# Attention block of a fused LayerNorm + attention + MoE kernel: half of the exponentials go through a fp16 copy on VectorE, and the projections get two PSUM slots each in place of four shared ones

## The chip, the cores and the metric

The kernel runs on all 8 NeuronCores of one Trainium2 chip. Each core takes two of the 16 sequences (4096 tokens) and works alone; no data goes between cores. The metric is the device time in microseconds of the slowest core. Engines are called by the names of the profile: PE (TensorE, matmul), PEld (its weight loads), DVE (VectorE), ACT (ScalarE), POOL (GpSimd) and SP (SyncE); the last two only issue DMAs here.

## The reference

```python
b, s, d_in = x.shape                    # 16, 2048, 1024; 16 heads of 64
q = (x @ Wq.T) ...; k = (x @ Wk.T) ...; vv = (x @ Wv.T) ...
scores = jnp.einsum('bhid,bhjd->bhij', q, k)
scores = scores + jnp.einsum('bhid,ijd->bhij', q, R)          # R: sin/cos of (j - i)
scores = scores + jnp.einsum('hd,bhjd->bhj', u, k)[:, :, None, :]
scores = scores + jnp.einsum('hd,ijd->hij', v, R)[None]
attn = jax.nn.softmax(scores, axis=-1)
ctx = jnp.einsum('bhij,bhjd->bhid', attn, vv)
s = ctx @ Wo.T + bo

gate_logits = xs @ Wg                                          # 8 experts, top 2
h = jax.nn.relu(jnp.einsum('td,edf->etf', xs, W1) + b1)        # d_ff 4096
out_e = jnp.einsum('etf,efd->etd', h, W2) + b2
...
xn = layernorm(x); out = x + attention(xn) * silu(moe(xn))
```

## The kernel before

**Stages.** For each of the two sequences (`b`) the kernel first runs `ln_gate_batch` and then `attention_batch`; after both it runs the MoE (all 8 experts on all tokens, `w1_stage` at L828 and `w2_stage` at L874) and a last stage that joins the two results. Engines follow the program order of their own queue; each wait is a semaphore wait that is written by hand. P, A and V count what PE, ACT and DVE have finished.

**LayerNorm and gate (16 tiles of 128 tokens).** A tile is normalised on DVE, split into a high and a low bf16 part, transposed by PE 128 columns at a time (L307), and brought back to SBUF by ACT (L311, `xnT`) and DVE (L317). 24 small matmuls give the gate logits; a chain of tiny DVE operations and two sigmoids on ACT turn them into the weights `g_wgt` (L374). PE transposes `g_wgt` one tile later, after the next tile's transposes (L327), and ACT copies the result to `wgt_b` (L330).

**Attention, per head pair `hp_i` (8 of them).** (1) K projection: four chunks `ic` of 512 tokens, 8 matmuls each (L465), into `psA_` (ic 0, 1) and `psB_` (ic 2, 3); ACT copies the even head's 64 rows to `Kbuf[0]` (L475), DVE the odd head's to `Kbuf[1]` (L479). (2) `emit_pend`: the previous block's context is normalised (below). (3) DVE prepares `vt` (L485 to L490). (4) Q projection into the same four halves (L505); ACT copies each to one of two buffers `q_sb2` (L517), and DVE makes the rotated query from it, a *rope chain* of ten instructions (L522 to L538) that ends with the last reader of that buffer. (5) On even `hp_i` the V projection of four heads: 16 times 8 matmuls (L560), with ACT copies to `vaug` (L572, L575). Its weights `wvq` come by DMA on the SP queue from `wvbf_hbm`, a bf16 copy of Wv that POOL's first large DMA made in HBM.

**A block.** The four blocks `bi` of a head pair are (head, half of the queries). Each has 16 steps `jt`: scores (two matmuls of 512 columns, L609, into psA for even jt and psB for odd jt), the exponential on ACT over 1024 columns from PSUM (L632), and the context product (two matmuls, L636, into psC or psD in turn). PE's order is scores 0, scores 1, then for each jt: wait for exp(jt), context(jt), scores(jt+2). After step 15 DVE takes the reciprocal of the row sums (L652, one partition by 1024) and ACT copies the context to `ctx_stage` (L657). `emit_pend` broadcasts the reciprocal with two matmuls (L417) and multiplies on DVE (L425); it is called in the next block at jt = 10, or behind the next K projection.

```python
for jt in range(16):
    if jt == 10 and ("pend",) in last:
        emit_pend()
    ...
    p.wait("tensor", A, a_e_l[jt])
    ...
    if jt + 2 < 16:
        pe_s_l[jt + 2] = s_mm(jt + 2)
```

The first block of a head pair waits for rope chains 0 and 1, and for the ACT copy of chunk 3; the second block waits for rope chain 3 (L600 to L603).

## Time and profile before

| what | value |
|---|---|
| time, median of 2 runs | 10926.86 us (10899.97 to 10953.74) |
| profiled execution, its own time | 10124.97 us |
| span of its slowest core (core 2) | 10123.4 us |
| spans of the 8 cores | 10084.0 to 10123.4 us |
| mean granted TensorE clock of the cores | 0.956 to 0.959 |
| PE busy | 8893.5 us (88%) |
| DVE busy | 3470.5 us (34%) |
| ACT busy | 2875.3 us (28%) |

The profiled execution is 802 us (7.3%) below the median of the runs. Every row below comes from the profiled execution, so durations and sums are its own. The span is what lies between the first and the last instruction of the slowest core; it misses 1.6 us of the execution's time. The share of an engine is over the whole span, in which the MoE takes the larger part.

### The profile page before, as it was taken

The page shows a single profiled execution, that of the slowest core. Times are in us where ns is not written, and L with a number is a line of the kernel's source. Part 1 is how long each engine was busy: PE and PEld are TensorE (multiplying, and loading weights), DVE is VectorE, ACT ScalarE, POOL GpSimd, SP SyncE. Part 2 cuts the span into 40 slices and gives each one's busy share as a digit, 9 for nine tenths or more (in the row PEclk, how much of TensorE's full clock was granted, in tenths as well). Part 3 has the DMA queues.
Part 4 walks back from the last instruction along what each step waited for, and adds up shares of the span by engine and source line. Part 5 has one row for each costly group of instructions (what it writes and reads, how often), then busy time and mean ns, then how long its engine had stood idle before and what let it go on. Part 6 is the DMA issues. An engine that isn't in the chain of part 4 may idle for free.

```text
span 10123.4 us, 114688 instructions; the slowest of 8 cores (10084.0 to 10123.4 us)
## 1 busy us (share of the span) xinstructions
PE 8893.5 (88%) x41248; PEld 3938.4 (39%) x41248; DVE 3470.5 (34%) x4945; ACT 2875.3 (28%) x4394; POOL 69.1 (1%) x88
## 2 busy tenths in 40 slices
PE   1577753777789999999999999999999999999995
PEld 1222222222234444444444444444444444444443
DVE  3454444454412222222232222223222322322223
ACT  2466634666421111111112111111211111111111
POOL 0000000000000000000000000000000000000000
PEclk9999976999889999999999999999999999999997
DMA  3000011000032232222223222222322222222215
GB/s 67 30 3 1 1 34 40 3 1 1 24 64 55 59 67 55 55 55 55 56 56 73 55 55 55 55 55 55 67 60 57 57 55 55 55 60 66 55 38 175
DMA packets 381242, 500.10 MB, mean 49 GB/s; under 512 B 10432, under 2 KB 297280, under 8 KB 380632
## 3 DMA queue, kind: packets, MB, share of 16 engines
q1 hardware_dynamic: 308096, 340.04, 10.7%
q0 software_dynamic: 72608, 152.72, 9.7%
q8 instruction: 357, 5.85, 0.2%
q14 instruction: 181, 1.48, 0.0%
HBM read 603.31 MB, written 35.72 MB: 63 GB/s over the span
## 4 chain that ended last, share of the span: by engine, by line
PE 81%; ACT 7%; DVE 6%; issue 3%; DMA 1%; another core or an unknown queue 1%; DVEq 0%; ACTq 0%; SPq 0%; POOLq 0%
PE psH L828 35%; PE psO L874 35%; ACT exp L632 6%; PE psA L609 2%; PE psC L636 2%; PE psD L636 2%; PE psC L560 1%; DMA xo_t<-x 1%; DVE rope L527 1%; PE psB L609 1%; PE psA L465 1%; PE psA L676 1%; PE psB L676 0%; PE psA L307 0%
## 5 line engine op out<-in xcount | busy, mean ns | idle before, releaser
L828 PE MATMUL psH<-xn_tc,W1q 128*128 128x512 bf16 x16384 | 3603.5, 381 | 0.0
L874 PE MATMUL psO<-h_w,W2q 128*128 128x512 bf16 x16384 | 3577.5, 379 | 0.0
L844 ACT ACTIVATE h_sb<-psH,b_c 128x512 bf16<-128x512 f32 x2048 | 1296.7, 684 | 5592.5 <-PE psH L828 5592.5
L828 PEld LDWEIGHTS psH<-xn_tc,W1q 128*128 128x128 bf16 x16384 | 1609.5, 98 | 1958.5 <-issue 60.8
L874 PEld LDWEIGHTS psO<-h_w,W2q 128*128 128x128 bf16 x16384 | 1604.4, 98 | 1936.6 <-issue 15.7
L884 DVE TENSOR_TENSOR acc<-acc,psO 128x1024 bf16<-128x1024 bf16 x1024 | 1250.6, 1221 | 2150.6 <-PE psO L874 2148.0
L848 DVE TENSOR_TENSOR h_w<-h_sb,w_sb 128x512 bf16<-128x512 bf16 x2048 | 870.3, 425 | 2942.4 <-ACT h_sb L844 2939.6
L632 ACT ACTIVATE exp<-psA,cst 128x1024 bf16<-128x1024 f32 x512 | 569.5, 1112 | 157.2 <-PE psA L609 154.9
L632 ACT ACTIVATE exp<-psB,cst 128x1024 bf16<-128x1024 f32 x512 | 567.1, 1108 | 20.3 <-PE psB L609 18.3
L307 PE MATMUL psA<-ident_s,xnhi 128*128 128x128 bf16 x128 | 33.9, 265 | 468.1 <-DVE xnlo L295 374.5
L609 PE MATMUL psA<-Qbuf,Kbuf 128*128 128x512 bf16 x1024 | 311.8, 387 | 141.4 <-ACT q_sb L517 133.0
L636 PE MATMUL psC<-exp,vaug 128*65 128x512 bf16 x1024 | 312.2, 386 | 140.3 <-ACT exp L632 138.5
L636 PE MATMUL psD<-exp,vaug 128*65 128x512 bf16 x1024 | 304.1, 378 | 142.6 <-ACT exp L632 141.4
L652 DVE RECIPROCAL rec_row<-psC 1x1024 bf16<-1x1024 f32 x32 | 209.7, 6552 | 359.0 <-PE psC L636 359.0
L609 PE MATMUL psB<-Qbuf,Kbuf 128*128 128x512 bf16 x1024 | 310.0, 385 | 0.0
L652 DVE RECIPROCAL rec_row<-psD 1x1024 bf16<-1x1024 f32 x32 | 209.7, 6552 | 167.4 <-PE psD L636 167.4
L560 PE MATMUL psC<-wvq,xnT 128*128 128x256 bf16 x1024 | 134.3, 293 | 117.8 <-ACT vaug L572 117.8
L636 PEld LDWEIGHTS psC<-exp,vaug 128*65 128x65 bf16 x1024 | 75.1, 110 | 376.6 <-issue 376.6
L636 PEld LDWEIGHTS psD<-exp,vaug 128*65 128x65 bf16 x1024 | 72.0, 108 | 371.3 <-issue 371.3
L307 PEld LDWEIGHTS psA<-ident_s,xnhi 128*128 128x128 bf16 x128 | 13.3, 104 | 485.3 <-issue 483.9
L609 PEld LDWEIGHTS psA<-Qbuf,Kbuf 128*128 128x128 bf16 x1024 | 97.5, 97 | 263.8 <-issue 164.2
L527 DVE TENSOR_TENSOR rope<-tmpX,psD 32x512 f32<-32x512 bf16 x256 | 175.1, 684 | 27.7 <-DVE rope L527 1.4
(120 smaller groups left out, 2485.4 us busy)
## 6 DMA issues: line engine op xcount, KB each, us to landing
xn_tc<-xnT_scr SPq DMA_DIRECT2D x256, 1024.0 KB, 5.7
W1q<-w POOLq DMA_DIRECT2D x32, 2048.0 KB, 17.9
W2q<-w POOLq DMA_DIRECT2D x32, 2048.0 KB, 34.1
xt<-x SPq DMA_DIRECT2D x32, 512.0 KB, 3.3
xo_t<-x SPq DMA_DIRECT2D x32, 512.0 KB, 12.1
out<-out_t SPq DMA_DIRECT2D x32, 512.0 KB, 11.4
xnT_scr<-xnT POOLq DMA_DIRECT2D x2, 4096.0 KB, 18.3
sT_scr<-Qbuf SPq DMA_DIRECT2D x16, 512.0 KB, 4.0
```

Of the source, the lines that this page charges most:

```text
L465: E.matmul(_ps[:, _o:_o + 512], wkT_b[:, _dt * D + _h * 128:_dt * D + (_h + 1) * 128], xnT[:, _dt * S + _ic * 512: _dt * S + (_ic + 1) * 512],
L527: p.op("vector", lambda E, _ro=r_out, _xs=xs_, _ys=ys_: E.tensor_tensor(rope[_ro:_ro + 32, :], tmpX[_xs:_xs + 32, :], psD_[_ys:_ys + 32, 0 ...
L560: E.matmul(psC_[:, _c:_c + 256], xnT[:, _dt * S + _jt * 128: _dt * S + (_jt + 1) * 128], _w[:, _dt * 256:(_dt + 1) * 256], start=(_dt == 0 ...
L609: E.matmul(_sl[:, _nh * 512:(_nh + 1) * 512], _K[:, _jt * 128:(_jt + 1) * 128], _Q[:, _ig * 1024 + _nh * 512: _ig * 1024 + (_nh + 1) * 512 ...
L632: E.activation(_eb[:], _sl[:], AF.Exp, bias=cst[:, 1:2]))
L636: E.matmul(_pc[0:65, _nh * 512:(_nh + 1) * 512], _va[:, _jt * 65:(_jt + 1) * 65], _eb[:, _nh * 512:(_nh + 1) * 512], start=(_jt == 0), sto ...
L652: E.reciprocal(rec_row[_par][:], _pc[64:65, :]))
L828: E.matmul(_ps[:, _sub * 512:(_sub + 1) * 512], _W[:, _dt * 1024 + _ft * 128:_dt * 1024 + (_ft + 1) * 128], _xb[:, _dt * 512:(_dt + 1) * 512],
L844: E.activation(_hb[:], _ps[:, _sub * 512:(_sub + 1) * 512], AF.Relu, bias=_bb[:, _fq * 8 + _ft:_fq * 8 + _ft + 1]))
L848: E.tensor_tensor(_hw[:, _ft * 512:(_ft + 1) * 512], _hb[:], w_sb[:, _tc * 512:(_tc + 1) * 512], ALU.mult))
L874: E.matmul(_ps[:, _sub * 512:(_sub + 1) * 512], _W[:, _ft * D + _dmt * 128:_ft * D + (_dmt + 1) * 128], _hw[:, _ft * 512:(_ft + 1) * 512], ...
L884: E.tensor_tensor(acc.ap().rearrange("p (dmt t) -> p dmt t", dmt=NDT)[:, _dmg * 2:_dmg * 2 + 2, _tc * 512:(_tc + 1) * 512], acc.ap().rearr ...
```

## The change

The change touches the start, the LayerNorm stage and attention; the MoE and the last stage stay as they are.

- The exponential of odd `jt` is made in two steps: DVE copies the 1024 score columns from PSUM to a fp16 tile `exq` (two of them in turn), and ACT reads that tile. PE still waits for the exponential, as before. Even `jt` is unchanged.
- The K projection uses only the two halves of psA, the Q projection only the two halves of psB. The third and fourth chunk of each wait for the copies of the first and second.
- `q_sb` is one buffer. The copy of the next chunk waits for the whole rope chain of the chunk before.
- The first block of a head pair waits for all four rope chains.
- The HBM copy of Wv is gone. `wvq` is loaded on POOL's queue straight from the f32 input, with the conversion in the DMA.
- The transposition of `g_wgt` and its copy stand at the end of their own tile, not in the next.

```diff
-            p.dma("gpsimd", wvbf_hbm, wvT_d, svb)
...
                     vwg = p.op("vector", lambda E: E.scalar_tensor_tensor(
                         g_wgt[:], g_msk2[:], g_w2[:, 0:1], g_t4[:], ALU.mult, ALU.add), V)
-                    last[("pW",)] = (tt, vwg)
+                    p.wait("tensor", V, vwg)
...
+                    peW = p.op("tensor", lambda E: E.transpose(psW, g_wgt[:], ident[:]), P)
...
             def wv_load(b, qi):
-                p.wait("sync", svb, 16)
                 if ("wvu", qi % 2) in last:
-                    p.wait("sync", P, last[("wvu", qi % 2)])
+                    p.wait("gpsimd", P, last[("wvu", qi % 2)])
                 last[("wvl", qi % 2)] = p.dma(
-                    "sync", wvq[qi % 2].ap().rearrange("p (dt n) -> p dt n", dt=NDT),
-                    wvbf_hbm.rearrange("(dt p) n -> p dt n", p=128)[:, :, qi * 256:(qi + 1) * 256],
+                    "gpsimd", wvq[qi % 2].ap().rearrange("p (dt n) -> p dt n", dt=NDT),
+                    wvT_d.rearrange("(dt p) n -> p dt n", p=128)[:, :, qi * 256:(qi + 1) * 256],
                     svq[qi % 2])
...
                     for ic in range(4):
-                        ps_kq = psA_ if ic < 2 else psB_
-                        off = (ic % 2) * 512
-                        if ("psKQ", ic) in last:
-                            a_c, v_c = last[("psKQ", ic)]
...
+                        half = ic % 2
+                        if ("psKA", half) in last:
+                            a_c, v_c = last[("psKA", half)]
+                            p.wait("tensor", A, a_c)
+                            p.wait("tensor", V, v_c)
...
-                        if ("q_sb", ic % 2) in last:
-                            p.wait("scalar", V, last[("q_sb", ic % 2)])
+                        if ("q_sb",) in last:
+                            p.wait("scalar", V, last[("q_sb",)])
...
                         if bi == 0:
-                            p.wait("tensor", A, max(a_v_done, a_q_l[3]))
-                            p.wait("tensor", V, max(v_q_ic[1], v_ones))
+                            p.wait("tensor", A, a_v_done)
+                            p.wait("tensor", V, max(v_q_done, v_ones))
                             p.wait("tensor", DG, kb_DG)
-                        if bi == 1:
-                            p.wait("tensor", V, v_q_ic[3])
...
-                            p.wait("scalar", P, pe_s_l[jt])
-                            if ("expw", jt % 2) in last:
-                                p.wait("scalar", P, last[("expw", jt % 2)])
-                            a_e_l[jt] = p.opf("scalar", lambda E, _eb=eb, _sl=sl:
-                                              E.activation(_eb[:], _sl[:], AF.Exp, bias=cst[:, 1:2]))
+                            if jt % 2 == 0:
...
+                            else:
+                                xq = exq[(jt // 2) % 2]
+                                p.wait("vector", P, pe_s_l[jt])
+                                if ("exq", (jt // 2) % 2) in last:
+                                    p.wait("vector", A, last[("exq", (jt // 2) % 2)])
+                                v_ca = p.opf("vector", lambda E, _xq=xq, _sl=sl:
+                                             E.tensor_copy(_xq[:], _sl[:]))
+                                p.wait("scalar", V, v_ca)
+                                if ("expw", 1) in last:
+                                    p.wait("scalar", P, last[("expw", 1)])
+                                a_e_l[jt] = p.opf("scalar", lambda E, _eb=eb, _xq=xq:
+                                                  E.activation(_eb[:], _xq[:], AF.Exp, bias=cst[:, 1:2]))
+                                last[("exq", (jt // 2) % 2)] = a_e_l[jt]
                             p.wait("tensor", A, a_e_l[jt])
```

Two places of the engines' order are shown as rows of the program. A row is one instruction (or xN equal ones in sequence) with its line, its output and inputs, and what it waits for; line numbers of the changed kernel are its own.

DVE in the first head pair, from the end of the last rope chain to the end of the third block, before:

```order
L538 TENSOR_SCALAR Qbuf<-q_sb,ucol_s 64x512 [waits V]
L652 RECIPROCAL rec_row<-psC 1x1024 [waits P]
L425 TENSOR_TENSOR ctx_buf<-ctx_stage,psC 64x1024 [waits P]
L652 RECIPROCAL rec_row<-psD 1x1024 [waits P]
L425 TENSOR_TENSOR ctx_buf<-ctx_stage,psD 64x1024 [waits P]
L652 RECIPROCAL rec_row<-psC 1x1024 [waits P]
```

The same place of DVE in the changed kernel:

```order
L506 TENSOR_SCALAR Qbuf<-q_sb,ucol_s 64x512 [waits V]
L605 CAST exq<-psB 128x1024 [waits P] x2
L605 CAST exq<-psB 128x1024 [waits P,A] x6
L631 RECIPROCAL rec_row<-psC 1x1024 [waits P]
L605 CAST exq<-psB 128x1024 [waits P,A] x5
L405 TENSOR_TENSOR ctx_buf<-ctx_stage,psC 64x1024 [waits P]
L605 CAST exq<-psB 128x1024 [waits P,A] x3
L631 RECIPROCAL rec_row<-psD 1x1024 [waits P]
```

Eight copies a block now share DVE's queue with the reciprocal of the block before, which stands ahead of the first of them, and with the multiplication of `emit_pend`, which stands between the fifth and the sixth.

ACT from the end of head pair 0 into head pair 1, before (psA and psB of the K and Q projections, then the first exponentials):

```order
L657 ACTIVATE ctx_stage<-psD 64x1024 [waits P,V]
L475 ACTIVATE Kbuf<-psA 64x512 [waits P] x2
L475 ACTIVATE Kbuf<-psB 64x512 [waits P] x2
L517 ACTIVATE q_sb<-psA 128x512 [waits P,V] x2
L517 ACTIVATE q_sb<-psB 128x512 [waits P,V] x2
L632 ACTIVATE exp<-psA,cst 128x1024 [waits P]
L632 ACTIVATE exp<-psB,cst 128x1024 [waits P]
```

The same place of ACT in the changed kernel:

```order
L636 ACTIVATE ctx_stage<-psD 64x1024 [waits P,V]
L451 ACTIVATE Kbuf<-psA 64x512 [waits P] x4
L486 ACTIVATE q_sb<-psB 128x512 [waits P,V] x4
L598 ACTIVATE exp<-psA,cst 128x1024 [waits P]
L610 ACTIVATE exp<-exq,cst 128x1024 [waits V,P]
```

ACT's number of instructions is the same; K now passes through psA alone and Q through psB alone, and every second exponential waits for DVE in addition to PE.

## Rows read from the trace of the kernel before

**Rows 1.** Stages: stretch, length, busy us (instructions) per engine, clock, DMA share, GB/s

```profile
core 2: us, PE busy (x) PEld busy (x) DVE busy (x) ACT busy (x) POOL busy (x), PEclk, DMA share, GB/s
83.90:339.00 255.10, 59.79 (x656) 39.52 (x656) 123.53 (x361) 90.59 (x237) 0.00 (x0) 1.00 0.08 27
339.00:1417.00 1078.00, 789.62 (x3392) 304.00 (x3392) 517.00 (x543) 651.22 (x865) 0.93 (x1) 0.93 0.03 9
...
2785.00:10017.00 7232.00, 7168.22 (x32952) 3231.26 (x32952) 2132.16 (x3080) 1373.11 (x2180) 56.39 (x67) 0.99 0.25 57
```

**Rows 2.** Timeline of head pair 0, block 0: start us, us, engine, line, operation

```profile
391.49 0.59 PE L636 MATMUL psC<-exp,vaug 128*65 128x512 bf16 x2 [0.41 <-ACT exp L632]
...
391.92 0.59 PE L609 MATMUL psA<-Qbuf,Kbuf 128*128 128x512 bf16 x2
...
392.67 1.11 ACT L632 ACTIVATE exp<-psA,cst 128x1024 bf16<-128x1024 f32 x1 [0.32 <-PE psA L609]
...
393.92 0.59 PE L636 MATMUL psC<-exp,vaug 128*65 128x512 bf16 x2 [0.41 <-ACT exp L632]
```

**Rows 3.** Groups of instructions: count, busy us, mean ns, idle before

```profile
L884 DVE TENSOR_TENSOR acc<-acc,psO 128x1024 bf16<-128x1024 bf16 x1024 | 1250.6, 1221 | 2150.6 <-PE psO L874 2148.0 <-PE psO L911 2.6
...
L283 ACT ACTIVATE cols<-cols,cst 128x1 f32<-128x1 f32 x32 | 9.4, 294 | 91.5 <-DVE cols L280 91.1
```

**Rows 4.** Timelines, block ends in head pair 0 (first and third boundary)

```profile
407.38 0.59 PE L636 MATMUL psC<-exp,vaug 128*65 128x512 bf16 x2 [0.69 <-ACT exp L632]
...
408.08 6.55 DVE L652 RECIPROCAL rec_row<-psC 1x1024 bf16<-1x1024 f32 x1 [25.38 <-PE psC L636]
...
471.44 1.02 ACT L657 ACTIVATE ctx_stage<-psD 64x1024 bf16<-64x1024 f32 x1 [0.89 <-PE psD L636]
```

**Rows 5.** Timeline around jt = 10 of block 1, head pair 0

```profile
421.41 0.59 PE L609 MATMUL psB<-Qbuf,Kbuf 128*128 128x512 bf16 x2
...
422.65 1.21 DVE L425 TENSOR_TENSOR ctx_buf<-ctx_stage,psC 64x1024 bf16<-64x1024 bf16 x1 [8.02 <-PE psC L417]
```

**Rows 6.** Timelines of DVE, ACT and PE in head pair 1, projections and block 0

```profile
477.88 1.21 DVE L479 CAST Kbuf<-psA 64x512 bf16<-64x512 f32 x2
...
487.45 0.42 DVE L522 TENSOR_TENSOR tmpX<-q_sb,tcc_s 128x512 bf16<-128x512 bf16 x1
...
493.98 0.35 DVE L538 TENSOR_SCALAR Qbuf<-q_sb,ucol_s 64x512 bf16<-64x512 bf16 x1
...
494.42 0.60 ACT L517 ACTIVATE q_sb<-psB 128x512 bf16<-128x512 f32 x1 [11.33 <-DVE Qbuf L538]
501.40 0.60 ACT L517 ACTIVATE q_sb<-psB 128x512 bf16<-128x512 f32 x1 [6.38 <-DVE Qbuf L538]
...
502.35 1.01 PE L609 MATMUL psA<-Qbuf,Kbuf 128*128 128x512 bf16 x2 [16.55 <-ACT q_sb L517]
...
523.77 0.59 PE L636 MATMUL psC<-exp,vaug 128*65 128x512 bf16 x2 [0.50 <-ACT exp L632]
```

**Rows 7.** Timelines of ACT and PE in head pair 2, with the V projection

```profile
618.19 0.60 ACT L517 ACTIVATE q_sb<-psB 128x512 bf16<-128x512 f32 x1 [6.38 <-DVE Qbuf L538]
...
635.10 0.59 PE L609 MATMUL psA<-Qbuf,Kbuf 128*128 128x512 bf16 x2 [1.03 <-ACT vaug L575]
```

**Rows 8.** Start: DMA issues (us to landing) and timeline at PE's first matmul

```profile
wqT_b<-wqT POOLq DMA_DIRECT2D x1, 2048.0 KB, 41.0
wkT_b<-wkT POOLq DMA_DIRECT2D x1, 2048.0 KB, 58.9
...
83.90 0.26 PE L307 MATMUL psA<-ident_s,xnhi 128*128 128x128 bf16 x1 [83.90 <-DMA Kbuf<-pab]
```

**Rows 9.** Timeline between two tiles of the gate stage

```profile
288.84 0.23 DVE L374 SCALAR_TENSOR_TENSOR g_wgt<-g_msk,g_w,g_t 128x8 bf16<-128x8 f32 x1
...
291.05 1.28 ACT L283 ACT_TABLE_LOAD   x1 [3.07 <-DVE cols L280]
```

**Rows 10.** Timeline of PE in the output projection of the first sequence

```profile
1405.23 3.30 PE L676 MATMUL psA<-ctx_buf,woT_b 128*128 128x512 bf16 x8 [3.25 <-DVE Qbuf L686]
1408.36 1.89 PE L676 MATMUL psB<-ctx_buf,woT_b 128*128 128x512 bf16 x8
```

More of the change, by code:

```diff
@@ L8 @@
 F32 = mybir.dt.float32
+F16 = mybir.dt.float16
 BF16 = mybir.dt.bfloat16
@@ L207, in build @@
             vt = sb2("vt", (128, S), BF16)
-            q_sb2 = [sb2(f"q_sb{i}", (128, 512), BF16) for i in range(2)]
+            q_sb = sb2("q_sb", (128, 512), BF16)
             tmpX = sb2("tmpX", (128, 512), BF16)
@@ L211, in build @@
             exp_sb = [sb2(f"exp{i}", (128, 1024), BF16) for i in range(2)]
+            exq = [sb2(f"exq{i}", (128, 1024), F16) for i in range(2)]
             rec_row = [sb2(f"rec_row{i}", (1, 1024), BF16) for i in range(2)]
@@ L491, in attention_batch @@
                             vt[:, _i * 512:(_i + 1) * 512], vt[:, _i * 512:(_i + 1) * 512], tmpX[:], ALU.subtract))
-                    a_q_l = [None] * 4
-                    v_q_ic = [None] * 4
                     for ic in range(4):
-                        ps_kq = psA_ if ic < 2 else psB_
-                        off = (ic % 2) * 512
-                        a_c, v_c = last[("psKQ", ic)]
-                        if a_c is not None:
-                            p.wait("tensor", A, a_c)
-                        if v_c is not None:
-                            p.wait("tensor", V, v_c)
+                        half = ic % 2
+                        if ("psQB", half) in last:
+                            p.wait("tensor", A, last[("psQB", half)])
                         pe_q = None
                         for dt in range(NDT):
-                            mk = (lambda E, _dt=dt, _h=hp_i, _ic=ic, _ps=ps_kq, _o=off:
-                                  E.matmul(_ps[:, _o:_o + 512],
+                            mk = (lambda E, _dt=dt, _h=hp_i, _ic=ic, _ph=half:
+                                  E.matmul(psB_[:, _ph * 512:(_ph + 1) * 512],
                                            wqT_b[:, _dt * D + _h * 128:_dt * D + (_h + 1) * 128],
```

85 lines of the change are left out of this document (30 added, 55 removed).

## The prediction

> **What bounds the kernel now.** I read the stages first, then the timeline of one block, then its ends. The stages [rows 1] show two regimes. From 2785 to 10017 us PE is busy for 7168 of 7232 us: the MoE is bound by matmuls, and the change does not touch it. From 339 to 1417 us (and again, with the same counts, for the second sequence) PE is busy for 790 of 1078 us and ACT for 651: nobody is full, so attention is bound by a chain of waits. The timeline of a block [rows 2] names it. PE starts a context product at 391.49 and scores 0.43 us later; ACT starts the exponential 0.75 us after the scores started, and PE starts the next context product of that parity 1.25 us after the exponential started. 0.43 + 0.75 + 1.25 = 2.43 us, and the two steps jt and jt+1 share that period. ACT's two exponentials of some 1.0 us each fit into it with 0.3 to 0.4 us to spare. So a pair of steps costs the length of one slot's loop, and whatever is put in series with either slot lengthens every pair.
>
> **The exponential by way of DVE (512 times).** The loop of the odd slot becomes: context to scores 0.43, scores to copy 0.75 (DVE and ACT start alike after PE), the copy, the handoff to ACT, the exponential to the next context. The trace has no copy of this shape; the nearest row is DVE's 1221 ns for 128x1024 with a PSUM operand [rows 3], and the casts of 64x512 take 1.21 us for two [rows 6], so 1.22 is my value, with half of it (0.6) as the lower end, if fp16 went at twice the rate, and 1.3 as the upper one. The handoff: the last reader ends at 493.98 + 0.35 = 494.33 and ACT starts at 494.42, 0.09 us [rows 6]. The exponential from SBUF is not in the trace either. One column with a bias takes 294 ns from SBUF [rows 3]; ACT's slope is (1.02 - 0.60) / 512 = 0.82 ns a column [rows 4, 6], so 1.13 us against 1.11; I add 0.03. The loop is 0.43 + 0.75 + 1.22 + 0.09 + 1.28 = 3.77 us. PE's order does not let the even slot run on: context(jt+1) waits for the exponential of the odd step and scores(jt+2) and (jt+3) stand around it. A pair costs 3.77 in place of 2.43 us.
>
> **The reciprocal in DVE's queue.** Count from the last context product of a block, 407.38 [rows 4]. The reciprocal starts at +0.70 and takes 6.55 us, to +7.25. Before, the next block's exponentials ran beside it. Now the first copy of that block stands behind it: copy from 7.25 to 8.47, exponential at 8.56, context(1) at 9.84. Seven more pairs give 26.39. At jt = 10 the multiplication of `emit_pend` stands ahead of the sixth copy: the scores of step 11 start at 421.41, so their copy could start at 422.16, but the multiplication runs from 422.65 to 423.86 [rows 5], 1.70 us late. Context(15) comes at 9.84 + 26.39 + 1.70 = 37.9. Before, three such blocks took 471.44 - 408.07 = 63.4 us (the first context copy starts with the reciprocal), 21.1 each. +16.8 us, in 3 blocks of each of 16 head pairs: 48 x 16.8 = 807 us.
>
> **The first block of a head pair.** No reciprocal is in its way: scores at 0, copy at 1.18 to 2.40, exponential at 2.49, context(1) at 3.77, context(15) at 3.77 + 26.39 = 30.2, plus about 1.3 for the slow clock with which the block starts now too. Before: 523.77 - 502.35 = 21.4 [rows 6]. +10.0, 16 times: 161 us.
>
> **K, Q, V projections.** Before, all four chunks of K ran without a wait, and DVE's casts began at 477.88, behind the reciprocal [rows 6]. With two halves the third chunk starts only behind the first cast, at about 478.6, and the fourth cast ends near 483.1; the `vt` operations and the first rope chain follow it, 2.8 us later than the 487.45 of [rows 6]. With one `q_sb` the copy of the next chunk waits for the chain: a chain takes 494.33 - 487.45 = 6.88, and then 0.09 + 0.60 for the copy and its handoff, 7.6 us from chain to chain in place of 6.98. And the first block waits for the end of the fourth chain, not for the copy of chunk 3 behind the second: 487.45 + 2.8 + 3 x 7.6 + 6.88 + 0.3 = 520.2 against 502.35 [rows 6]. +17.9 us on the 8 odd head pairs, 143 us. On even ones the V projection stands behind the copy of chunk 3 in ACT's queue: from that copy to the first scores is 635.10 - 618.19 = 16.9 us [rows 7], longer than the last chain, so only the copy's delay counts: 3 x 7.6 - 2 x 6.98 - 0.6 = 8.2, and 2.8 more where a reciprocal is ahead (6 of 8). 6 x 11.0 + 2 x 8.2 = 82 us. What hid the last two chains was the first block; that cover is gone.
>
> **Start and weights of V.** PE's first matmul waits for the last DMA of POOL's queue, at 83.90. The weight matrices land one by one, 58.9 - 41.0 = 18 us apart [rows 8]. One of that size goes: -20 us, between 0 (if another load sets the start) and -24 (then the first tile's LayerNorm does). The later loads of `wvq` are a quarter of a matrix, about 5 us each, behind the store of `xnT`; in the first head pair PE wants them after the longer Q projection, so 0, up to 5 us a sequence.
>
> **The gate's transposition.** PE now waits for `g_wgt` at the end of its own tile, and next in its queue are transposes that need DVE's whole next tile, behind `g_wgt` on DVE. ACT's copy falls between 288.84 + 0.23 and 291.05, when ACT waits for DVE anyway [rows 9]. Cost 0, within 5 us either way. If that cover were gone it would be 0.3 us a tile.
>
> **The clock.** In the output projection PE idles for 3.25 us; the next 8 matmuls take 3.30 us, and the 8 after them 1.89 [rows 10]: the clock had fallen to its lower level (1.2 GHz), and to come back cost 1.4 us. The changed block leaves PE idle from about +3.7 to +9.8 behind each of 48 boundaries. I add 1.3 each, 60 us; the bounds are 0 and the rival below.
>
> **Sum.** 807 + 161 + 143 + 82 - 20 + 60 = 1233 us. On the profiled execution's own 10125 us that makes 11358. The runs shown have a median of 10926.86, 802 us more. No row of the trace holds that difference; I take it to be in the MoE, which is most of the time and bound by PE's clock, and carry it over: 12160 us, +11.3%.
>
> **Rivals.**
> - *The clock stays low through the blocks.* In a loop of 3.77 us PE has 4 x 0.43 = 1.7 us of work (46%), and it has fallen silent for 6 us before. Rows at either level: 8 matmuls take 1.4 us longer at the lower one, at most 0.2 each, and four stand in the loop, so a pair costs 0.8 more. 512 x 0.8 = 410, less the 60 already in: 11708, or 12510. For it: a gap of 3.25 us was enough [rows 10]. Against it: attention now has a granted clock of 0.93 [rows 1] with loops that have a gap each, and at the lower clock PE would be busy for 3.4 of 4.6 us, which should bring it back. The Trainium skill ("TensorE: Matmul & The Clock Gate", A second HAM failure mode: psum-queue depth-cycling) describes a kernel whose short idles between groups of matmuls made the gate go back and forth; by that rule this rival happens in part. The trace agrees for single gaps only.
> - *The copy is cheap.* If it takes 0.6 us in place of 1.22, a pair costs 3.15: 512 x 0.62 = 317 less, 11041, or 11843. Against it: no row shows DVE reading f32 from PSUM at more than about one column a cycle of the 1221 ns row.
> - *Not slower: the copy frees the slot.* Its place is PE's queue in the block. The copy, not the exponential, is the last reader of psB, so scores(jt+2) could be made while ACT still works. If PE ran ahead, the pair would cost ACT's time, 2.0 us in place of 2.43: 512 x 0.4 = 205 us gained, and the reciprocal would be absorbed too. With +225 for projections and -20 for the start that is 10125, no change, 10927. It decides only if the scores stand ahead of the wait in PE's queue; by the code they do not, as context(jt) with its wait on the exponential comes first.
>
> **How the numbers follow.** The forecast gets 0.70, the low clock 0.18, the cheap copy 0.09, the freed slot 0.03. The range reaches from below the cheap copy to the low clock: 11700 to 12560 us. A measurement of this kernel can tell about 2% from no change; faster 0.01, same 0.02, slower 0.97.
>
> **What would show it.** In the changed profile: the copy near 1.22 us and 512 of them; exponentials of odd steps 3.77 us apart; block ends 37.9 us apart; PE idle for some 6 us behind each boundary, ended by an exponential that itself waited for a copy behind the reciprocal; ACT's copies of Q 7.6 us apart; the first matmul near 64 us; the MoE as long as before. Attention should last about 600 us more for each sequence. I am wrong if pairs cost well under 3.5 us, if the copies do not wait for the reciprocal, or if the granted clock in attention is far under 0.9.

## The result, and the profile after

The changed kernel is slower: the ratio of its time to that of the kernel before is 1.1427, with a 95% interval of 1.1348 to 1.1505. In most executions of either kernel (seven of ten before, both runs shown among them, and nine of twelve of the changed one) the cores of one half of the chip (0 to 3 or 4 to 7), or of both, show a lower granted clock and take longer; the ratio, and the times below where nothing else is said, are from executions or halves without that, here called undisturbed.

| what | before | after |
|---|---|---|
| undisturbed executions | 10105 to 10107 us | 11515 to 11581 us |
| profiled execution, its own time | 10124.97 us | 11524.26 us |
| spans of the 8 cores | 10084.0 to 10123.4 us | 11499.7 to 11522.5 us |
| mean granted clock of the cores | 0.956 to 0.959 | 0.892 to 0.897 |
| DVE busy | 3470.5 us | 4097.5 us |

From profile to profile that is +1399 us. The forecast was +1233 us on the profiled execution, which makes 11358; but it named 12160 as the time, because it carried over the 802 us by which the two runs shown lay above the profile. The undisturbed executions of the kernel before are all within 20 us of the profile. The time that came, 11524 us, is below the range's 11700. As a ratio, +11.3% was named (11358 to 10125 would be +12.2%), and +14.3% came.

The page of the changed kernel, with the clock of TensorE in 40 slices and the chain that ended last:

```profile
span 11522.5 us, 115392 instructions; the slowest of 8 cores (11499.7 to 11522.5 us)
...
PE 9291.0 (81%) x40476; PEld 4053.9 (35%) x41248; DVE 4097.5 (36%) x5457; ACT 2893.5 (25%) x4394; POOL 75.5 (1%) x95
...
PEclk9776776667777779999999999999999999999997
...
PE 73%; DVE 12%; ACT 7%; issue 6%; DMA 1%; another core or an unknown queue 1%; DVEq 0%; ACTq 0%; SPq 0%; POOLq 0%
```

A slice is 288 us; LayerNorm and attention of both sequences fill the first fifteen, and all of these but the first show a six or a seven for the clock. On the chain DVE has 12%, where it had 6% before.

The stages by windows, of the slowest core (core 0), to be read beside [rows 1]. The first is the LayerNorm of the first sequence, the second and third are attention of each sequence, the last is the MoE and the final stage:

```profile
63.40:319.00 255.60, 60.93 (x656) 39.57 (x658) 123.50 (x361) 90.79 (x237) 0.00 (x0) 1.00 0.09 27
319.00:2120.00 1801.00, 1012.34 (x3334) 362.38 (x3390) 830.38 (x799) 659.01 (x865) 4.45 (x5) 0.73 0.02 6
...
2390.00:4212.00 1822.00, 1014.53 (x3334) 364.08 (x3390) 831.13 (x800) 659.21 (x865) 8.57 (x11) 0.73 0.03 7
4212.00:11420.00 7208.00, 7118.28 (x32298) 3228.50 (x32955) 2133.02 (x3080) 1373.43 (x2180) 56.38 (x67) 0.99 0.23 58
```

Attention of the second sequence in the kernel before, which [rows 1] leave out:

```profile
1687.00:2785.00 1098.00, 790.79 (x3392) 304.04 (x3392) 517.76 (x544) 649.18 (x865) 5.50 (x7) 0.92 0.04 12
```

Attention went from 1078 to 1801 us in the first sequence (+723) and from 1098 to 1822 in the second (+724), and its granted clock from 0.93 and 0.92 to 0.73. LayerNorm and the MoE stayed (7232 and 7208 us in these windows; cores of one execution differ by as much there: from the first matmul behind attention, L788, to the end it is 7311 us on core 0 of before and 7338 on core 2). So the cost is 1447 us of attention, less 20 us at the start: 1427, and the 28 by which core 0 of the one is quicker in the MoE than core 2 of the other give the 1399. Taken core by core, the first matmul behind attention comes 1403 to 1429 us later than before, 1415 in the mean.

The block. First a pair of steps at the higher clock (matmuls of 0.59 us for two), then one at the lower (1.03), then a boundary between two blocks; timeline of all engines:

```profile
445.02 0.59 PE L615 MATMUL psD<-exp,vaug 128*65 128x512 bf16 x2 [1.38 <-ACT exp L610]
445.45 0.59 PE L574 MATMUL psB<-Qbuf,Kbuf 128*128 128x512 bf16 x2
446.22 1.23 DVE L605 CAST exq<-psB 128x1024 f16<-128x1024 f32 x1 [2.64 <-PE psB L574]
447.60 1.15 ACT L610 ACTIVATE exp<-exq,cst 128x1024 bf16<-128x1024 f16 x1 [1.72 <-DVE exq L605]
448.89 0.59 PE L615 MATMUL psD<-exp,vaug 128*65 128x512 bf16 x2 [2.27 <-ACT exp L610]
...
421.52 1.03 PE L615 MATMUL psD<-exp,vaug 128*65 128x512 bf16 x2 [1.14 <-ACT exp L610]
422.35 1.06 PE L574 MATMUL psB<-Qbuf,Kbuf 128*128 128x512 bf16 x2
423.58 1.23 DVE L605 CAST exq<-psB 128x1024 f16<-128x1024 f32 x1 [3.50 <-PE psB L574]
426.25 1.03 PE L615 MATMUL psD<-exp,vaug 128*65 128x512 bf16 x2 [1.14 <-ACT exp L610]
...
406.85 0.59 PE L615 MATMUL psC<-exp,vaug 128*65 128x512 bf16 x2 [2.27 <-ACT exp L610]
407.54 6.55 DVE L631 RECIPROCAL rec_row<-psC 1x1024 bf16<-1x1024 f32 x1 [2.14 <-PE psC L615]
414.13 1.23 DVE L605 CAST exq<-psB 128x1024 f16<-128x1024 f32 x1
415.50 1.15 ACT L610 ACTIVATE exp<-exq,cst 128x1024 bf16<-128x1024 f16 x1 [5.95 <-DVE exq L605]
416.79 1.03 PE L615 MATMUL psD<-exp,vaug 128*65 128x512 bf16 x2 [6.07 <-ACT exp L610]
...
449.58 1.02 ACT L636 ACTIVATE ctx_stage<-psD 64x1024 bf16<-64x1024 f32 x1 [0.83 <-PE psD L615]
```

The first pair is 448.89 - 445.02 = 3.87 us long: 0.43 to the scores, 0.77 to the copy, 1.38 to the exponential (which starts 0.15 us behind the copy's end), 1.29 to the context product. The second, at the lower clock, is 426.25 - 421.52 = 4.73 us: the scores start 0.40 later behind the context product, the copy 0.46 later behind the scores, and the rest is the same. At the boundary the reciprocal takes DVE first, the copy starts when it ends, and PE stands for 6.07 us. ACT's copies of the context at the two ends of this block start at 407.54 and 449.58: 42.0 us, where before it was 21.1 [rows 4]. The mean of all 48 blocks that follow another is 42.0 as well.

The groups:

```profile
L605 DVE CAST exq<-psB 128x1024 f16<-128x1024 f32 x512 | 626.6, 1224 | 1339.1 <-PE psB L574 1337.1
L610 ACT ACTIVATE exp<-exq,cst 128x1024 bf16<-128x1024 f16 x512 | 587.5, 1147 | 1325.8 <-DVE exq L605 1223.8 <-PE psA L574 102.0
L598 ACT ACTIVATE exp<-psA,cst 128x1024 bf16<-128x1024 f32 x512 | 561.3, 1096 | 77.3 <-PE psA L574 75.9 <-PE psB L574 1.4
```

ACT now stands for 1326 us ahead of the exponentials of odd steps, nearly all of it for DVE; those of even steps wait for next to nothing (77.3 us in all), because their scores are ready while the odd loop runs.

The start and the projections: PE's first matmul, the third and fourth chunk of K, which wait for their slots, ACT's copies of the third chunk of K and of Q, and the first scores of an odd head pair:

```profile
63.41 0.27 PE L306 MATMUL psA<-ident_s,xnhi 128*128 128x128 bf16 x1 [63.41 <-DMA Kbuf<-pab]
...
541.33 5.30 PE L441 MATMUL psA<-xnT,wkT_b 128*128 128x512 bf16 x16 [4.25 <-DVE Kbuf L455]
...
544.13 0.59 ACT L451 ACTIVATE Kbuf<-psA 64x512 bf16<-64x512 f32 x1 [6.37 <-PE psA L441]
...
569.29 0.60 ACT L486 ACTIVATE q_sb<-psB 128x512 bf16<-128x512 f32 x1 [7.14 <-DVE Qbuf L506]
...
584.92 0.58 PE L574 MATMUL psA<-Qbuf,Kbuf 128*128 128x512 bf16 x1 [19.06 <-DVE Qbuf L506]
```

The start is 83.90 - 63.41 = 20.5 us earlier, still behind the last DMA of POOL's queue. The copies of Q are 7.74 us apart, and PE stands for 19 us until the fourth rope chain is through.

### The profile page after: what moved, and what is told of

Read it like the earlier page. It is cut to its first block, busy times and chain, and to the rows that moved or that the text cites. A ratio compares the mean times of both kernels' runs of the same rounds, so it can differ in the third digit from the quotient of the medians.

```text
span 11522.5 us, 115392 instructions; the slowest of 8 cores (11499.7 to 11522.5 us)
## 1 busy us (share of the span) xinstructions
PE 9291.0 (81%) x40476; PEld 4053.9 (35%) x41248; DVE 4097.5 (36%) x5457; ACT 2893.5 (25%) x4394; POOL 75.5 (1%) x95
## 4 chain that ended last, share of the span: by engine, by line
PE 73%; DVE 12%; ACT 7%; issue 6%; DMA 1%; another core or an unknown queue 1%; DVEq 0%; ACTq 0%; SPq 0%; POOLq 0%
PE psH L807 31%; PE psO L853 31%; ACT exp L610 5%; DVE exq L605 5%; PE psB L574 3%; PE psD L615 2%; PE psC L615 2%; DVE rope L495 1%; PE psA L441 1%; PE psC L527 1%; DMA xo_t<-x 1%; DVE rec_row L631 1%; PE psA L655 0%; PE psB L655 0%
## 5 line engine op out<-in xcount | busy, mean ns | idle before, releaser
L807 PEld LDWEIGHTS psH<-xn_tc,W1q 128*128 128x128 bf16 x16384 | 1607.6, 98 | 1951.9 <-issue 33.2
L605 DVE CAST exq<-psB 128x1024 f16<-128x1024 f32 x512 | 626.6, 1224 | 1339.1 <-PE psB L574 1337.1
L610 ACT ACTIVATE exp<-exq,cst 128x1024 bf16<-128x1024 f16 x512 | 587.5, 1147 | 1325.8 <-DVE exq L605 1223.8
L615 PE MATMUL psD<-exp,vaug 128*65 128x512 bf16 x1024 | 427.5, 510 | 585.4 <-ACT exp L610 553.2
L615 PE MATMUL psC<-exp,vaug 128*65 128x512 bf16 x1024 | 412.0, 493 | 496.6 <-ACT exp L610 464.2
L598 ACT ACTIVATE exp<-psA,cst 128x1024 bf16<-128x1024 f32 x512 | 561.3, 1096 | 77.3 <-PE psA L574 75.9
L574 PE MATMUL psA<-Qbuf,Kbuf 128*128 128x512 bf16 x960 | 410.2, 514 | 172.5 <-DVE Qbuf L506 153.6
L615 PEld LDWEIGHTS psD<-exp,vaug 128*65 128x65 bf16 x1024 | 102.8, 133 | 894.4 <-issue 894.2
L574 PE MATMUL psB<-Qbuf,Kbuf 128*128 128x512 bf16 x1000 | 410.0, 499 | 2.9 <-issue 2.2
L475 PE MATMUL psB<-xnT,wqT_b 128*128 128x512 bf16 x502 | 141.0, 440 | 157.4 <-ACT q_sb L486 156.9
L574 PEld LDWEIGHTS psA<-Qbuf,Kbuf 128*128 128x128 bf16 x1024 | 127.0, 125 | 364.7 <-issue 320.3
```

The costliest lines, as they stand in the source:

```text
L574: E.matmul(_sl[:, _nh * 512:(_nh + 1) * 512], _K[:, _jt * 128:(_jt + 1) * 128], _Q[:, _ig * 1024 + _nh * 512: _ig * 1024 + (_nh + 1) * 512 ...
L598: E.activation(_eb[:], _sl[:], AF.Exp, bias=cst[:, 1:2]))
L605: E.tensor_copy(_xq[:], _sl[:]))
L610: E.activation(_eb[:], _xq[:], AF.Exp, bias=cst[:, 1:2]))
L615: E.matmul(_pc[0:65, _nh * 512:(_nh + 1) * 512], _va[:, _jt * 65:(_jt + 1) * 65], _eb[:, _nh * 512:(_nh + 1) * 512], start=(_jt == 0), sto ...
L807: E.matmul(_ps[:, _sub * 512:(_sub + 1) * 512], _W[:, _dt * 1024 + _ft * 128:_dt * 1024 + (_ft + 1) * 128], _xb[:, _dt * 512:(_dt + 1) * 512],
```

## Experiments

They ask three things: whether the cost splits as the sum says, whether the clock or the chain of waits is in the pairs, and whether the way in which the change could have paid (a copy that frees the slot) exists.

The mean length of a block in each of them, in us, on one core. For a block that follows another it is the time between ACT's copies of the context; for the first block of a head pair, from its first exponential to that copy:

| kernel | 48 blocks behind another | 16 first blocks |
|---|---|---|
| before (core 2) | 21.1 | 21.0 |
| changed (core 0) | 42.0 | 33.2 |
| e1, the copy alone (core 5) | 41.8 | 39.2 |
| e2, all but the copy (core 0) | 21.1 | 21.2 |
| e3, reciprocal in pieces (core 1) | 35.2 | 32.9 |
| e5, scores ahead, before (core 7) | 20.7 | 20.7 |
| e6, scores ahead, changed (core 0) | 33.4 | 23.6 |
| e7, e6 with e3 (core 2) | 27.9 | 23.5 |
| e8, more matmuls (core 0) | 39.6 | 31.7 |
| e9, e5 with a third tile (core 2) | 18.5 | 18.2 |

### The parts alone

**e1.** The kernel before, with nothing but the copy of odd steps (with one fp16 tile in place of two).

```diff
-                            p.wait("scalar", P, pe_s_l[jt])
+                            if jt % 2 == 0:
...
+                            else:
+                                p.wait("vector", P, pe_s_l[jt])
+                                if ("exq", 0) in last:
+                                    p.wait("vector", A, last[("exq", 0)])
+                                v_ca = p.opf("vector", lambda E, _xq=xq, _sl=sl:
+                                             E.tensor_copy(_xq[:], _sl[:]))
+                                p.wait("scalar", V, v_ca)
```

> The kernel before with only the exponential of odd steps changed (copy on DVE to one fp16 tile, ACT reads it); projections, q_sb, gate and Wv stay as before. My theory (the copy lies in the loop of the odd slot, and the reciprocal ahead of it in DVE's queue): a pair costs 3.87 us at the full clock and 4.73 at the lower one, block ends 41 to 42 us apart, profiled execution about 11400 us, that is 1285 above the 10125 of before. It is not simply 11524 minus the projections' share, because here rope chains 2 and 3 stand ahead of the first block's copies. Rival (the projections carry most of the loss): under 10600.

Measured: cores of 11369.5 to 11389.5 us, granted clock 0.895 to 0.899. The same four cores took 10088.4 to 10104.5 us with the kernel before on the same chip, so the copy alone costs 1274 to 1291 us, as expected. That is not its share in the changed kernel: first blocks take 39.2 us here and 33.2 there. The odd head pairs make the difference (44 to 46 us against 32 to 35 in the even ones): there two rope chains still stand ahead of the first block's copies in DVE's queue. 16 times 6.0 are 96 us, and without them some 1190 are left.

**e2.** The changed kernel with the exponential path of before: only start, gate, K, Q and V are changed.

```diff
-                            if jt % 2 == 0:
...
-                                v_ca = p.opf("vector", lambda E, _xq=xq, _sl=sl:
-                                             E.tensor_copy(_xq[:], _sl[:]))
...
+                            p.wait("scalar", P, pe_s_l[jt])
+                            if ("expw", jt % 2) in last:
+                                p.wait("scalar", P, last[("expw", jt % 2)])
```

> The changed kernel with the exponential of before (ACT reads PSUM on all 16 steps); all other parts of the change stay. My theory: only the projections and the start are left, 225 - 20, so 10330 us, odd head pairs' first scores some 18 us and even ones' 8 to 11 us later; granted clock in attention back near 0.9. Rival (the rest costs nothing, the copy is all): 10105 to 10150.

Measured: 10350.48 us, clock 0.948 to 0.950, where 10330 was expected. From here to the changed kernel, which differs by the copy alone, it is 1174 us, 84% of the 1399 and close to the 1190 of e1. PE on core 4, with the wait ahead of an odd pair's first scores:

```profile
512.43 1.01 PE L574 MATMUL psA<-Qbuf,Kbuf 128*128 128x512 bf16 x2 [19.41 <-DVE Qbuf L506]
```

The blocks are 21.0 to 21.3 us long (context copies at 397.93, 418.92, 439.97, 461.29), as before. From the last context product of one head pair to the first scores of the next it takes 51.6 to 53.0 us on most crossings where the next pair is odd (50 on a few), against 31.7 in the kernel before, and 61.1 to 61.5 against 48.2 to 48.4 where it is even. That is mostly +20 to +21 and +13 us, where the forecast had +17.9 and +8.2 to +11.0. The first matmul behind attention comes 224 to 251 us later than on the same core before, 240 in the mean of the eight; with the 20 us of the start, the projections cost 260 us and not 225.

**e3.** The changed kernel with the reciprocal in four pieces of 256 columns, one behind each of the next block's first four copies.

```diff
                                 v_ca = p.opf("vector", lambda E, _xq=xq, _sl=sl:
                                              E.tensor_copy(_xq[:], _sl[:]))
+                                do_rec(1)
                                 p.wait("scalar", V, v_ca)
...
+                        for qk in range(4):
+                            rq.append(lambda _pc=ps_c, _par=par, _k=qk: p.opf("vector", lambda E:
+                                      E.reciprocal(rec_row[_par][:, _k * 256:(_k + 1) * 256],
+                                                   _pc[64:65, _k * 256:(_k + 1) * 256])))
```

> The changed kernel with the reciprocal in four pieces of 256 columns, one behind each of the next block's first four copies. My theory: a piece of some 1.7 us fits into the 2.6 us that DVE has free between copies, so copy 1 of a block comes 5.6 us earlier, 48 times: 270 us less, 11250, and up to 50 more less if the clock falls less often without the idle time of 6 us. Rival (the reciprocal's 6.5 us are only moved, DVE is too full): within 60 us of 11524.

Measured: cores of 11187.0 to 11213.0 us, clock 0.915 to 0.919: 310 us less than the changed kernel, where 270 to 320 were expected. Core 1, DVE at the boundary:

```profile
408.32 1.22 DVE L621 CAST exq<-psB 128x1024 f16<-128x1024 f32 x1 [4.36 <-PE psB L590]
409.57 1.75 DVE L647 RECIPROCAL rec_row<-psC 1x256 bf16<-1x256 f32 x1
412.19 1.22 DVE L621 CAST exq<-psB 128x1024 f16<-128x1024 f32 x1 [0.86 <-PE psB L590]
413.44 1.75 DVE L647 RECIPROCAL rec_row<-psC 1x256 bf16<-1x256 f32 x1
```

A piece ends 0.86 us ahead of the next copy, so the reciprocal costs nothing any more. In the changed kernel PE has 48 waits of 5.2 to 6.1 us behind boundaries, 270 us together, and here it has none of over 3.1; the rest goes with the clock, which is low less often: of this core's intervals between exponentials of odd steps 255 are under 4.1 us and 176 between 4.1 and 4.9, and the granted clock of its first attention stage is 0.79 in place of 0.73.

### The clock in the pairs

In the changed kernel's core 0 the intervals between odd exponentials fall into two heaps: 193 under 4.1 us (186 of them at 3.9) and 199 between 4.1 and 4.9 (185 at 4.7); the rest hold a boundary, a projection or the multiplication. What the clock cost had to be tried with more work on PE and no other change.

**e4.** Even scores three times over, and thirteen times at the first step of the second to fourth block of a head pair.

```diff
+                                if jt % 2 == 0:
+                                    for _f in range(12 if (jt == 0 and bi > 0) else 2):
+                                        pe_s_l[jt + 2] = s_mm(jt + 2)
```

> The changed kernel with the scores of even steps made three times in place of once (same result, written again while PE would idle; 13 times at the first step of blocks 1 to 3). Theory that PE's idle time lowers the clock: granted clock in attention rises from 0.72 to over 0.9, nearly all pairs last 3.87 us (now 193 of them do and 199 last 4.73), and the time falls by some 170 to 230 us to about 11320, with more work on PE. Rival (the slow pairs come from something other than PE's idle time, as the power of eight cores): pairs stay mixed and the time stays or rises.

Measured: in one of three executions (12989.18 us) the four cores of one half are undisturbed, with 11373.0 to 11382.1 us at a clock of 0.946 to 0.947. That is some 135 us under the changed kernel's 11499.7 to 11522.5, less than the 170 to 230 expected. The profile comes from another execution, so its loops are not read here.

**e8.** The same with less: even scores twice, and seven times at the first step of those blocks.

```diff
+                                if jt % 2 == 0:
+                                    for _f in range(6 if (jt == 0 and bi > 0) else 1):
+                                        pe_s_l[jt + 2] = s_mm(jt + 2)
```

> As e4 with less filler: scores of even steps twice, 7 times at the first step of blocks 1 to 3. Theory that PE's idle time lowers the clock: in the loop of 3.87 us PE has work for 2.15 in place of 1.72 us, and the idle time of 6 us is cut to 3. Granted clock in attention over 0.85, at least three quarters of the pairs at 3.87 us, time 11350 to 11400. Rival (not the idle time): as the changed kernel, 193 to 199 pairs at each pace, 11524 or more.

Measured: 11370.15 us, clock 0.937 to 0.939. Attention of the first sequence:

```profile
319.00:2060.00 1741.00, 1034.99 (x4007) 396.08 (x4080) 832.52 (x803) 660.79 (x866) 4.45 (x5) 0.87 0.03 7
```

One loop of it:

```profile
401.46 0.59 PE L615 MATMUL psC<-exp,vaug 128*65 128x512 bf16 x2 [1.41 <-ACT exp L610]
401.89 0.59 PE L574 MATMUL psB<-Qbuf,Kbuf 128*128 128x512 bf16 x2
402.46 0.59 PE L615 MATMUL psC<-exp,vaug 128*65 128x512 bf16 x2
402.89 1.02 PE L574 MATMUL psA<-Qbuf,Kbuf 128*128 128x512 bf16 x4
405.32 0.59 PE L615 MATMUL psC<-exp,vaug 128*65 128x512 bf16 x2 [1.41 <-ACT exp L610]
```

With more work the kernel is 154 us faster. The loop is 405.32 - 401.46 = 3.86 us, the same as without the extra matmuls, which lie in the gap; what changed is how often the loop is the short one: 326 intervals are under 4.1 us and 67 between 4.1 and 4.9. So the low clock was a cost of its own in the changed kernel, at least these 154 us (one execution; the half of e4 agrees in its sign and size). The blocks of the table hold 142 of them: 48 times 2.4 and 16 times 1.5.

### Scores ahead of the context product

**e5.** The kernel before, with scores(jt+2) in front of context(jt) in PE's queue.

```diff
                             p.wait("tensor", A, a_e_l[jt])
+                            if jt + 2 < 16:
+                                pe_s_l[jt + 2] = s_mm(jt + 2)
...
-                            if jt + 2 < 16:
-                                pe_s_l[jt + 2] = s_mm(jt + 2)
```

> The kernel before with one change of PE's order: scores(jt+2) stand ahead of context(jt), both behind the wait on exp(jt). If the pair of steps is a loop of waits (context 0.43, scores to exponential 0.75, exponential to PE 1.25), taking the context out of it leaves 2.0 us, at ACT's own 2.02: block ends 18.1 us apart in place of 21.1, some 190 us less, 9930 us, ratio 0.98. Rival (ACT's throughput bounds already): no change.

Measured: 10113.07 us beside 10125.9 of the kernel before on the same chip (22 us less in the mean of the eight cores), where 190 less were expected: a miss. ACT and PE of core 7 show why:

```profile
392.96 1.12 ACT L632 ACTIVATE exp<-psA,cst 128x1024 bf16<-128x1024 f32 x1 [0.59 <-PE psC L638]
...
394.22 0.59 PE L609 MATMUL psA<-Qbuf,Kbuf 128*128 128x512 bf16 x2 [0.23 <-ACT exp L632]
394.65 0.59 PE L638 MATMUL psC<-exp,vaug 128*65 128x512 bf16 x2
...
395.34 1.11 ACT L632 ACTIVATE exp<-psA,cst 128x1024 bf16<-128x1024 f32 x1
```

```profile
L632 ACT ACTIVATE exp<-psA,cst 128x1024 bf16<-128x1024 f32 x512 | 570.1, 1113 | 140.4 <-PE psD L638 59.6 <-PE psC L638 59.1 <-PE psA L609 17.8
```

From scores to exponential it is 395.34 - 394.22 = 1.12 us, not 0.75: it starts 0.10 us after the end of the context product, 394.65 + 0.59. In the group of these exponentials (second fence) the idle time ahead is put down to the context products in psC and psD for 118.7 of 140.4 us; before, 154.9 of 157.2 were the scores'. The exponential writes one of two `exp` tiles, and its last reader is the context product that now comes after the scores. One chain was shortened by 0.43 us and the other lengthened by 0.37; the 0.06 left are what a pair gained (2.38 us where it was 2.44), 30 us in 512 pairs.

**e6.** The changed kernel with scores(jt+2) ahead of context(jt) in all steps. In odd steps they wait for the copy alone and stand ahead of the wait on the exponential; in even ones they stand behind that wait, as in e5. This is the rival "the copy frees the slot".

```diff
-                            p.wait("tensor", A, a_e_l[jt])
+                            if jt % 2 == 1:
+                                if jt + 2 < 16:
+                                    p.wait("tensor", V, v_ca)
+                                    pe_s_l[jt + 2] = s_mm(jt + 2)
+                                p.wait("tensor", A, a_e_l[jt])
+                            else:
+                                p.wait("tensor", A, a_e_l[jt])
+                                if jt + 2 < 16:
+                                    pe_s_l[jt + 2] = s_mm(jt + 2)
...
-                            if jt + 2 < 16:
-                                pe_s_l[jt + 2] = s_mm(jt + 2)
```

> The changed kernel with PE's order changed so that the copy frees the slot: scores(jt+2) of odd steps wait for the copy alone and stand ahead of context(jt); scores of even steps stand ahead of context(jt) behind the same wait as now. If my account of the loop is right, pairs last 2.1 us (ACT's two exponentials of 1.05), what is left is the reciprocal ahead of each block and the projections: 10540 us. Rival (DVE's copy or PSUM access is a bound by itself, whatever the order): pairs stay over 3 us and the time over 11200.

Measured: 10937.9 to 10949.6 us on cores 0 to 3 of one execution, clock 0.925 to 0.926. That is some 565 us under the changed kernel, still 840 over the one before, and 400 over the 10540 that were expected: a miss. The trace is of another execution, in which core 0 took 10965.5 us. Its first blocks are 23.6 us long, 9.6 less than in the changed kernel and 2.6 over the kernel before. Those behind another block still take 9.8 us more than that, 470 us in 48: with this order too the copy stands behind the whole reciprocal. The pairs come at 2.6 us most often, not at 2.1. ACT's idle time ahead of the exponentials is put down to this:

```profile
L610 ACT ACTIVATE exp<-exq,cst 128x1024 bf16<-128x1024 f16 x512 | 587.5, 1148 | 684.9 <-DVE exq L605 594.1 <-PE psA L574 58.4 <-PE psD L623 15.3
L598 ACT ACTIVATE exp<-psA,cst 128x1024 bf16<-128x1024 f32 x512 | 563.9, 1101 | 141.6 <-PE psA L574 73.9 <-PE psD L623 40.8 <-PE psC L623 21.8
```

Ahead of the odd ones it is the copy (594.1 of 684.9 us), and only ahead of the even ones the context product, the last reader of the `exp` tile, has a part (62.6 of 141.6). So the tile of e5 holds little here. Which other wait keeps the pair at 2.6 us was not tried.

**e7.** e6 and the split reciprocal of e3 together.

```diff
+                                do_rec(1)
                                 p.wait("scalar", V, v_ca)
...
+                                if jt + 2 < 16:
+                                    p.wait("tensor", V, v_ca)
+                                    pe_s_l[jt + 2] = s_mm(jt + 2)
```

> As e6, with the reciprocal in four pieces behind the first four copies as in e3. Pairs at 2.1 us leave DVE only 0.9 us between copies, so the pieces of 1.7 us stretch the first four pairs to about 3 us each: 3.6 us a block in place of 5.6 of wait. 10450 us. If pieces fit as in e3: 10280. If the split gains nothing at this pace: 10540 or more.

Measured: 10731.28 us, clock 0.937 to 0.939, where 10450 was expected. The order in PE's queue and the reciprocal together give back 793 of the 1399 us, in a kernel that still makes all 512 copies; blocks behind another are 26.8 to 29.0 us long, 27.9 in the mean. The pieces are not free at this pace: a copy of 1.22 and a piece of 1.75 us fill DVE for the 3.0 us between copies, and such a block takes 4.4 us more than a first one. The kernel stays 600 us over the one before, 240 of them the projections less the start.

**e9.** What e5 lacked: the order of e5 in the kernel before, with a third `exp` tile.

```diff
-            exp_sb = [sb2(f"exp{i}", (128, 1024), BF16) for i in range(2)]
+            exp_sb = [sb2(f"exp{i}", (128, 1024), BF16) for i in range(3)]
...
-                            eb = exp_sb[jt % 2]
+                            eb = exp_sb[jt % 3]
```

> As e5 (the kernel before, scores ahead of context) with three exp tiles in place of two. e5 gained nothing because exp(jt+2) waits for context(jt), the reader of its tile, so the loop still held the context. Without that wait the loop is scores to exponential 0.75, exponential to PE 1.25: 2.0 us, at ACT's 2.02. Block ends 18.1 to 18.6 us apart in place of 21.1: 160 to 190 us less, ratio 0.982 to 0.985. Rival (some other wait or ACT's rate takes over): ratio over 0.995.

Measured: 9946.35 us; the kernel before took 10110.47 to 10115.63 in three executions on the same chip (a fourth took 10166.34), so the ratio is 9946 / 10111 = 0.984 from one execution. The undisturbed halves of its three others bear it out: their cores took 9915.5 to 9939.3 us, those of undisturbed executions and halves of the kernel before on that chip 10083.0 to 10114.1. Context copies start at 406.75, 425.16, 443.62 and 462.09, 18.4 us apart in place of 21.1. ACT, and the group of its even exponentials:

```profile
395.48 1.11 ACT L632 ACTIVATE exp<-psA,cst 128x1024 bf16<-128x1024 f32 x1
396.48 1.11 ACT L632 ACTIVATE exp<-psB,cst 128x1024 bf16<-128x1024 f32 x1
397.49 1.11 ACT L632 ACTIVATE exp<-psA,cst 128x1024 bf16<-128x1024 f32 x1
```

```profile
L632 ACT ACTIVATE exp<-psA,cst 128x1024 bf16<-128x1024 f32 x512 | 568.4, 1110 | 45.2 <-PE psA L609 43.7 <-PE psD L638 0.7 <-PE psC L638 0.5
```

One exponential starts every 1.00 us with no idle time between them, and the idle time ahead of those of psA is 45.2 us where it was 157.2: ACT has become the bound of the blocks.

**e10.** e9 with the start of the change: no HBM copy of Wv, `wvq` on POOL's queue from the f32 input.

```diff
-            p.dma("gpsimd", wvbf_hbm, wvT_d, svb)
...
-                    "sync", wvq[qi % 2].ap().rearrange("p (dt n) -> p dt n", dt=NDT),
-                    wvbf_hbm.rearrange("(dt p) n -> p dt n", p=128)[:, :, qi * 256:(qi + 1) * 256],
+                    "gpsimd", wvq[qi % 2].ap().rearrange("p (dt n) -> p dt n", dt=NDT),
+                    wvT_d.rearrange("(dt p) n -> p dt n", p=128)[:, :, qi * 256:(qi + 1) * 256],
```

> As e9, with the one part of the change that gains taken over: Wv straight from its f32 input on POOL's queue, no copy in HBM. Starts 20 us earlier: 20 us below e9, ratio about 0.981. If the later loads get in the way, as e9 or above.

Measured: 9928.06 us, 18 less than e9, and the fastest version: 9928 / 10111 = 0.982 of the kernel before, again one execution, with 9897.3 to 9917.8 us in the undisturbed halves of four others. It uses the one part of the change that pays.

## Why the prediction was wrong in its time and right in its direction

**The base, which failed.** The step reads: "No row of the trace holds that difference; I take it to be in the MoE, which is most of the time and bound by PE's clock, and carry it over: 12160 us". The difference belonged to the two executions and not to the kernel: undisturbed ones take 10105 to 10107 us, as the profile did. Its place was guessed right, as two cores of one execution of e1 show (core 3, then core 5, from the first matmul behind attention to the end):

```profile
4077.00:11657.00 7580.00, 7450.27 (x33152) 3311.55 (x33152) 2179.08 (x3112) 1393.89 (x2185) 56.34 (x67) 0.95 0.24 59
...
4064.00:11369.00 7305.00, 7178.67 (x33152) 3247.94 (x33150) 2177.82 (x3112) 1391.60 (x2185) 56.30 (x67) 0.98 0.24 61
```

The same instructions take 275 us more at a granted clock of 0.95 in place of 0.98. What failed is to forecast with it: a term that comes and goes from one execution to the next, on the base and hence on the whole range. Without it the range would have been 10898 to 11758 and have held the 11524; its middle, 11358, would still have been 166 us short.

**The copy's loop, right, 0.10 us short.** 3.77 us was forecast and 3.87 measured. The copy took 1.224 us (1.22), its handoff and the exponential's start were 1.38 in place of 1.31, and the rest was right to 0.03. The handoff is what was mis-sized, 0.15 us from DVE to ACT in place of 0.09. 512 times 0.10 are 51 us.

**The reciprocal, right.** PE stands for 6.07 us behind a boundary, ended by an exponential that waited for a copy behind the reciprocal, and e3 took 310 us away by splitting it. 37.9 us and 1.3 for the clock were forecast for a block; the first three of head pair 0 took 42.0, 41.3 and 42.9, the difference being pairs at the lower clock.

**The clock, right in kind and mis-sized.** "I add 1.3 each, 60 us; the bounds are 0 and the rival below" failed: the rival's loop, with 0.8 us more, is there in half of the pairs, at 0.86 us. 199 times 0.86 are 171 us, nearly three times the term; e8 gave back 154 with a sixth of the classified pairs still slow. The argument against the rival, that the clock would come back in such a loop, was half true: it does come back, and falls again. What makes it fall in one pair and not in the next was not tried. The granted clock of attention, for which 0.9 had been named as the limit, was 0.73. The Trainium skill ("TensorE: Matmul & The Clock Gate", A second HAM failure mode: psum-queue depth-cycling) describes a gate that goes back and forth where the engine idles shortly between groups of matmuls. The trace now agrees for a whole stage, with 193 pairs at the one level and 199 at the other.

**K, Q and V, right in kind, 35 us short.** 225 were forecast, e2 shows 260: mostly +20 to +21 us per odd pair in place of 17.9, +13 in place of 8.2 to 11.0. Chains are 7.74 us apart and not 7.6, 0.4 us a pair. The first chain comes 4.4 us later and not 2.8: in the changed kernel it starts at 554.58 behind a reciprocal at 534.09, before at 487.45 behind one at 471.40. The two chunks of K that wait for a slot are made partly at the lower clock: 16 matmuls take 5.30 us after PE stood for 4.25, the first 16 took 3.62. These two make 2.0 of the 2 to 3 us by which the odd pairs lie over their forecast; the even ones were not taken apart.

**Start, gate, MoE.** -20.5 us (-20), nothing, nothing.

The three shortfalls, 51 + 111 + 35 = 197 us, account for the 194 by which attention and start together (1427) lie above the forecast 1233. The blocks say the same: 48 times 20.9 and 16 times 12.2 are 1198 us, 170 over the 1028 (807 + 161 + 60) that were forecast for them. Of the rivals, the cheap copy is refuted by 1224 ns. "Not slower: the copy frees the slot" was right that the code forbids it, but its price, "the pair would cost ACT's time, 2.0 us", was not shown with the copy in place: in the kernel without it e5 changed the order and stayed at 2.38 us for want of a second tile, e9 added the tile and reached 2.01, but e6 with the copy has pairs of 2.6. And the reciprocal, which that rival held for absorbed, costs 9.8 us a block in e6. Whether the copy with three `exp` tiles and a split reciprocal would come down to ACT's time was not tried.

## What to carry to other kernels

Where no engine is full, count the loop: the time from one release to the next around the slot. An instruction put into that loop costs its full length each time, even on an engine that is idle for half of the stage (DVE, busy 517 of 1078 us before), and it inherits everything that stands ahead of it in its engine's queue. And before a loop's order is changed to free one buffer, list all readers of all buffers that the waiting instruction touches: with two `exp` tiles the new order gave 0.1%, with three 1.6%. Where the runs lie far above their own profile, a forecast should stand on the profile, with both bases inside its range: the difference may belong to the executions and not to the kernel.

## What the runs showed of the hardware that was not expected

- PE, busy for 4 x 0.43 = 1.72 us of a loop of 3.87 with gaps of up to 2.27, neither keeps its higher clock nor loses it for good: half of the pairs run at 2.4 GHz and half at 1.2. Two more matmuls in the gap (e8) raised the stage's granted clock from 0.73 to 0.87, and made the kernel 154 us faster by adding work.
- The exponential from the fp16 tile in SBUF takes 1147 ns, that from f32 in PSUM 1096 in the same kernel. Its smaller input saved nothing.
- A reciprocal over one partition by 1024 columns takes 6.55 us and one of 256 columns 1.75 (e3): it goes by columns, and a fourfold split costs 4 x 1.75 - 6.55 = 0.45 us of DVE.
